# A decoder layer on one core: four low halves of the expert weights made by VectorE, and the last reads and stores issued from two queues

## What is computed

```python
x = x + attn(layernorm(x), Wq, Wk, Wv, Wo, betas)              # 16 heads of 128, segments of 64, delta memory
x = x + xattn(layernorm(x), ctx_512, Wq, Wkv_expand, Wout)     # 16 heads of 16, causal
x = x + ffn(layernorm(x), gate_kernel, w0, w1, wo)             # 8 experts of 512, the best 2 for each token

# ffn
top_k_weights, top_k_indices = top_k(x @ gate_kernel, 2);  weights = softmax(top_k_weights)
out = sum over the 2 experts of  weight * ((silu(x @ w0[e]) * (x @ w1[e])) @ wo[e])
```

## Time and profile before

| | us |
|---|---|
| median of 3 runs (lowest, highest) | 561.98 (561.61, 562.02) |
| the profiled execution | 559.13 |
| its span, first to last instruction | 557.4 |
| TensorE busy in the span | 498.6 (89%) |
| VectorE busy | 355.7 (64%) |
| ScalarE busy | 320.2 (57%) |
| GpSimd busy | 144.1 (26%) |
| mean granted TensorE clock | 0.954 of full |

### The profile page before, as it was taken

One profiled execution on the slowest core, in us unless ns is written; L12 is line 12 of the kernel. 1 busy time (PEld: TensorE's weight loads), 2 busy tenths in 40 slices (PEclk: granted clock), 3 DMA queues, 4 the chain that ended last, 5 costly groups with the idle time before them and its releaser, 6 DMA issues. The chain is left out here.

```text
span 557.4 us, 11832 instructions
## 1 busy us (share of the span) xinstructions
PE 498.6 (89%) x4164; PEld 417.9 (75%) x4165; DVE 355.7 (64%) x782; ACT 320.2 (57%) x762; POOL 144.1 (26%) x141
## 2 busy tenths in 40 slices
PE   8989999999999999999899799996737999999960
PEld 3768888887898888888689667774624888888850
DVE  5367777776654777776666377777372666666654
ACT  4377777778626777777672389996203444444430
POOL 5110000003100000000000439998011455555530
PEclk9989999999999999999999899999559999999995
DMA  9421111111010111120000024443213355454527
GB/s 266 160 57 44 55 55 55 56 58 58 19 39 20 56 47 53 55 56 20 0 2 1 1 82 148 145 135 101 68 41 113 119 169 168 144 157 152 169 76 226
DMA packets 24001, 48.05 MB, mean 86 GB/s; under 512 B 2960, under 2 KB 11168, under 8 KB 23968
## 3 DMA queue, kind: packets, MB, share of 16 engines
q1 hardware_dynamic: 21120, 41.17, 24.2%
q0 software_dynamic: 2240, 6.04, 3.1%
q10 hardware_dynamic: 608, 0.39, 0.3%
HBM read 42.48 MB, written 5.11 MB: 85 GB/s over the span
## 5 line engine op out<-in xcount | busy, mean ns | idle before, releaser
L666 PE MATMUL psum<-a_xt_hi,a_qk_hi 128*128 128x512 f32 x128 | 54.6, 426 | 0.0
L1409 POOL DMA_INDIRECT picks_dram<-x_wout,e_pick_row x23 | 38.8, 1685 | 51.8 <-DVE x_wout L1572 51.8
L666 PE MATMUL psum<-a_xt_hi,a_qk_lo 128*128 128x512 f32 x128 | 50.6, 395 | 0.0
L666 PE MATMUL psum<-a_xt_lo,a_qk_hi 128*128 128x512 f32 x128 | 50.5, 394 | 0.0
L987 ACT ACTIVATE x_probs<-psum,x_neg_max 128x128 f32<-128x128 f32 x128 | 45.9, 406 | 6.7 <-DVE x_neg_max L1044 6.7
L1450 ACT ACTIVATE e_inner_hi<-psum 128x512 fp32r<-128x512 f32 x23 | 13.8, 599 | 57.7 <-PE psum L1632 57.7
L578 DVE COPY a_weights_t<-psum 64x256 f32<-64x256 f32 x32 | 13.7, 428 | 49.4 <-PE psum L782 49.4
L916 POOL MEMSET x_mask<- 128x512 bf16 x1 | 0.5, 525 | 167.5 <-POOLq L250 167.5
L444 ACT ACTIVATE a_probs<-a_shifted 128x256 f32<-128x256 f32 x32 | 13.4, 419 | 50.1 <-DVE a_shifted L544 50.1
L796 PE MATMUL psum<-a_weights_t,a_v 64*128 64x64 f32 x256 | 34.9, 275 | 8.0 <-issue 4.1
L1623 PE MATMUL psum<-expert_w_hi,e_x_hi 128*128 x92 | 38.3, 416 | 2.2 <-DVE e_x_lo L1550 2.2
(11 more groups left out here) (238 smaller groups left out, 1513.5 us busy)
## 6 DMA issues: line engine op xcount, KB each, us to landing
x_k_t<-in_expert_wo SPq DMA_DIRECT2D x23, 512.0 KB, 3.5
a_qk_raw<-in_wqk SPq DMA_DIRECT2D x32, 256.0 KB, 2.6
x_xn_t<-in_expert_w SPq DMA_DIRECT2D x16, 512.0 KB, 3.8
a_wv_raw<-in_wv SPq DMA_DIRECT2D x17, 256.0 KB, 2.7
x_sb<-in_x SPq DMA_DIRECT2D x2, 512.0 KB, 5.0
x_k_t<-in_wo SPq DMA_DIRECT2D x1, 1024.0 KB, 10.4
x_v<-in_wo SPq DMA_DIRECT2D x1, 1024.0 KB, 12.9
xn_dram<-xn SPq DMA_DIRECT2D x1, 1024.0 KB, 4.4
```

The lines of the kernel that those rows point to most:

```text
L666: last = pe.matmul(out, pick_l(left[a], k), pick_r(right[b], k), start=start and n == 0, stop=n == 3 * KD - 1, skip_group_check=not start)
L1409: pool.indirect_dma_start(out=picks_dram, out_offset=bass.IndirectOffsetOnAxis(ap=pick_row[:, tile:tile + 1], axis=0), in_=y_rows[:, slot, ...
```

## The change

It does two things.

1. VectorE makes the low halves of pieces 3, 7, 11 and 14. The table `VECTOR_PIECES` says at the end of which batch's `step` it does so: 2, 3, 5 and 6. VectorE waits for the piece's high half first (`w_hi_ready`), and counts `w_split_v` up. GpSimd still casts all 16 pieces and skips the subtraction of these four. SP waits for `w_split_v` where the buffer was last used by one of them.
2. At the end SP issues the reads of the first picks and the stores of the even batches; ScalarE issues the reads of the second picks and the stores of the odd batches. Both wait for `y_stored` first.

```diff
--- before.py
+++ after.py
@@ -819,6 +819,7 @@
 NE_WIDTH = 2 * KD * M
 PIECE = NE_WIDTH // 2
 PIECES = 2 * NE
+VECTOR_PIECES = {3: 2, 7: 3, 11: 5, 14: 6}
 CROSS_SCALE = 1.0 / float(HD) ** 0.5
 CH = NX // 2
 ROWG = 32
@@ -875,7 +876,7 @@
     var3_ready, std3_ready, ln3_chain, xn3_ready = sem("e_var_ready"), sem("e_std_ready"), sem("e_ln_chain"), sem("e_xn_ready")
     xt3_done, xt3_ready, logits_done = sem("e_xt_done"), sem("e_xt_ready"), sem("e_logits_done")
     w_loaded = [sem(f"e_w_loaded{i}") for i in range(2)]
-    w_hi_ready, w_split = sem("e_w_hi_ready"), sem("e_w_split")
+    w_hi_ready, w_split, w_split_v = sem("e_w_hi_ready"), sem("e_w_split"), sem("e_w_split_v")
     inv_spread, t_first_ready = sem("x_inv_spread"), sem("x_t_first_ready")
     pv_done, inv_ready, heads_ready = sem("x_pv_done"), sem("x_inv_ready"), sem("x_heads_ready")
     it_done, it_ready, y_done, y_added = sem("x_it_done"), sem("x_it_ready"), sem("x_y_done"), sem("x_y_added")
@@ -894,6 +895,13 @@
         for b in range(B):
             step(b)
 
+    def vector_pieces(n):
+
+        return sum(1 for piece in VECTOR_PIECES if piece < n)
+
+    def piece_cols(n):
+        return slice(n * PIECE, (n + 1) * PIECE)
+
     def q_banks(pair):
 
         return [c.bank[4 + 2 * (pair % 2) + k][:, 0:2 * S] for k in range(KD)]
@@ -907,8 +915,10 @@
 
             sp.wait_ge(q_done, B // 2)
             for n in range(PIECES):
-                if n >= 2:
-                    sp.wait_ge(w_split, n - 1)
+                if n - 2 in VECTOR_PIECES:
+                    sp.wait_ge(w_split_v, vector_pieces(n - 1))
+                elif n >= 2:
+                    sp.wait_ge(w_split, n - 1 - vector_pieces(n - 1))
                 sp.dma_start(xn_t[:, n % 2, :], c.expert_w[n // 2][:, (n % 2) * PIECE:(n % 2 + 1) * PIECE]).then_inc(w_loaded[n % 2], 16)
 
         @block.gpsimd
@@ -949,11 +959,12 @@
             pad_values(0)
             pad_values(1)
             for n in range(PIECES):
-                cols = slice(n * PIECE, (n + 1) * PIECE)
+                cols = piece_cols(n)
                 pool.wait_ge(w_loaded[n % 2], 16 * (n // 2 + 1))
                 pool.tensor_copy(c.expert_w_hi[:, cols], xn_t[:, n % 2, :]).then_inc(w_hi_ready, 1)
-                pool.wait_ge(w_hi_ready, n + 1)
-                pool.tensor_tensor(c.expert_w_lo[:, cols], xn_t[:, n % 2, :], c.expert_w_hi[:, cols], ALU.subtract).then_inc(w_split, 1)
+                if n not in VECTOR_PIECES:
+                    pool.wait_ge(w_hi_ready, n + 1)
+                    pool.tensor_tensor(c.expert_w_lo[:, cols], xn_t[:, n % 2, :], c.expert_w_hi[:, cols], ALU.subtract).then_inc(w_split, 1)
                 if n >= 2 and n % 2 == 0 and n // 2 + 1 < B:
                     pad_values(n // 2 + 1)
 
@@ -1058,6 +1069,14 @@
                 if b >= 1:
                     normalise(b - 1)
                 copy_weights(2 * b, 0)
+                for n, at in VECTOR_PIECES.items():
+                    if at == b:
+                        split_piece(n)
+
+            def split_piece(n):
+                dve.wait_ge(w_hi_ready, n + 1)
+                dve.tensor_tensor(c.expert_w_lo[:, piece_cols(n)], xn_t[:, n % 2, :], c.expert_w_hi[:, piece_cols(n)],
+                                  ALU.subtract).then_inc(w_split_v, 1)
 
             def copy_weights(u, ch):
 
@@ -1352,6 +1371,8 @@
 
         return left is None or left >= n
 
+    picks = picks_dram[0:PICKS * P, :].rearrange("(k b p) d -> k p b d", k=TOPK, b=B)
+
     with nc.Block() as block:
         @block.sync
         def _(sp):
@@ -1372,12 +1393,10 @@
             tiles(sp, step)
             for slot in range(2):
                 sp.wait_ge(y_stored[slot], 16 * ((TILES + 1 - slot) // 2))
-            picks = picks_dram[0:PICKS * P, :].rearrange("(k b p) d -> p k b d", k=TOPK, b=B)
             for b in range(B):
-                for k in range(TOPK):
-                    sp.dma_start(picked[k][:, b, :], picks[:, k, b, :]).then_inc(gathered[b], 16)
-            for b in range(B):
-                sp.wait_ge(mixed, TOPK * (b - b % 2) + 3 + b % 2)
+                sp.dma_start(picked[0][:, b, :], picks[0, :, b, :]).then_inc(gathered[b], 16)
+            for b in range(0, B, 2):
+                sp.wait_ge(mixed, TOPK * b + 3)
                 sp.dma_start(out[b], c.x_sb[:, b, :]).then_inc(out_stored, 16)
             sp.wait_ge(out_stored, 16 * B)
 
@@ -1455,6 +1474,13 @@
                     split_wo(tile + 1, 1 - slot, pair + slot)
 
             tiles(act, step)
+            for slot in range(2):
+                act.wait_ge(y_stored[slot], 16 * ((TILES + 1 - slot) // 2))
+            for b in range(B):
+                act.dma_start(picked[1][:, b, :], picks[1, :, b, :]).then_inc(gathered[b], 16)
+            for b in range(1, B, 2):
+                act.wait_ge(mixed, TOPK * (b - 1) + 4)
+                act.dma_start(out[b], c.x_sb[:, b, :]).then_inc(out_stored, 16)
 
         @block.vector
         def _(dve):
```

## The result

The changed kernel takes 573.24 us (median of 6 runs, 565.58 to 574.57) against 562.0 (median of 6, 560.22 to 568.57). The ratio is 1.0167 with a 95% interval of 1.0116 to 1.0218: 9.4 us slower. The medians are of all executions, while a ratio leaves out those more than 1.5% above the fastest of their kernel, so it is not the quotient of the medians (1.0200). The profiled execution took 568.86 (span 567.1) against 559.13.

What follows compares the result with a forecast made beforehand. Each batch's pace was set by a ring of ScalarE's exponentials, TensorE's transposes and scores, and VectorE's maximum. Delay 10.8, normalisations -2.2, clock +3.0, reads and stores -1.4: +10.2 on 562.0 gives 572.2 us, range 566.6 to 577.

Steps and rivals of the forecast that it cites:

- The waits: Cross attention: VectorE waits for GpSimd's casts, 6.5 us at piece 7 and 2.6 at piece 14; +10.8 us in all.
- The clock behind the holes: TensorE, idle at batches 3 and 6, falls to half clock: +3.0 us (2.0 and 1.0), bounds 0 and 5.4.
- Piece 11: VectorE's subtraction at batch 5 meets no wait for its cast and adds 0.4 us.
- What comes back: End of cross attention: GpSimd stops before the normalisations, so the first is no longer slowed from 0.41 to 2.57 us; -2.2.
- a mere 1 us of the low end: Allowance for a routing stage with TensorE's clock up, lowering the range's bottom from 567.6 to 566.6 us.
- The reads and stores: Kernel's end: two issuing queues let transfers pack, 12.4 of the 13.9 us remain; -1.4 us, bounds 0 and -3.0.
- The sum: Whole kernel: +11.6 us for VectorE's pieces and -1.4 for the end give +10.2, on the median 562.0: 572.2.
- "faster": Rival: piece 7's cast is ready by batch 3 through hidden slack in the loads; 559.4 or 557.4 us, chance 0.05.
- "The clock holds": Rival: VectorE's waits in cross attention occur but TensorE keeps full clock; 569.2 us, chance 0.17.
- "The port": Rival: VectorE's and GpSimd's subtractions block each other, up to 2.4 us at two places; 577 us, chance 0.06.
- "The tail gives nothing": Rival: splitting the final reads and stores gains nothing; 573.6 us, inside the range, no chance of its own.

Runs made afterwards that it cites:

- the filled holes: Changed kernel plus 16 and 7 unused TensorE products where TensorE idles behind VectorE's two waits; ratio 1.0156 (1.0067 to 1.0245).
- last-piece: Kernel before, but VectorE makes the low half of piece 15 alone, behind its last normalisation; reads and stores as before; ratio 0.989 (0.9843 to 0.9937).
- filled runs: Kernel before plus unused TensorE products (3, 2, 2 and 4) in its idle times at the end of cross attention; ratio 0.9977 (0.9938 to 1.0015).

## Why the prediction was right

It said 572.2 within 566.6 to 577.0, and 573.24 was measured. Step by step, each time behind the block's start, before and after:

| step | before | after | delay | forecast |
|---|---|---|---|---|
| maximum, batch 4 | 40.48 | 47.80 | 7.3 | 7.4 |
| maximum, batch 5 | 48.16 | 56.70 | 8.5 | 9.4 with 2.0 of clock |
| maximum, batch 6 | 55.83 | 64.59 | 8.8 | 9.8 |
| maximum, batch 7 | 63.50 | 75.16 | 11.7 | 12.8 |
| first normalisation | 76.23 | 88.92 | 12.7 | 13.8 with 1.0 more |
| block's end | 90.00 | 98.44 | 8.4 | 11.6 |

- **The waits** (6.5 and 2.6 forecast, 6.73 and 2.61 measured) were right, and so was the reason: when the cast ends, and when VectorE arrives. For piece 7 both are rows of before. For piece 14 the 2.6 is in part luck: VectorE arrived 71.41 behind the block's start (forecast 70.44, without the prediction's own clock term), and the cast ended at 73.98 (forecast 73.04), since the late loop held GpSimd at `pad_values(5)` and `pad_values(6)` already, and not at `pad_values(7)` alone. Both ends were 1.0 too early, and the difference stood.
- **The clock behind the holes** was taken at 3.0 and is 2.3 (1.24 and 1.06, by the filled holes). Piece 11 cost 0.2 instead of 0.4.
- **What comes back** was taken at 2.2 and is 4.25: 12.69 of delay went in, 8.44 came out. The term that was mis-sized is the clock of the gate's products. I had it as a mere 1 us of the low end. Before, half clock lasted from 389.5 to the block's end, 10.9 us; in the changed kernel it lasted from 401 to 404.5 and again from 407.9 to 410.6, 6.2 us. So some 2 us of the 4.25 go with the clock, beside the 2.2 of the normalisations; the last-piece and filled runs show that 3.5 to 4.3 hang on it in all.
- **The reads and stores** were taken at 1.4 (the working shown, 13.9 - 12.4, gives 1.5) and gave 0.7. The transfers did pack closer, to 13.20 us, but VectorE's adds close the chain: it waits 0.24, 1.18 and 0.28 us between the first pairs and then runs without a gap to 564.94. The median from issue to landing rose from 2.7 and 3.1 to 4.2 and 5.3 us; the likely reason, not tested, is that the reads of the first batches now share the DMA engines with those of the last. Why the third batch comes as late as 559.73 was not settled.
- **The sum** was 3.2 too high in the block and 0.7 too low at the end. By the traces the change costs 8.4 - 0.7 = 7.7, beside 0.3 in the experts and 1.7 of clock ahead of it; by the ratio 9.4; the forecast was 10.2. That the median came within 1.0 us of 572.2 is partly luck: the executions' spread is as large as what separates these.

Of the rivals, "faster" failed at the point it named: `w_hi_ready` of piece 7 was 6.7 us late. "The clock holds" is false; it fell behind both holes, though its 569.2 lies inside the range too, and only the trace tells them apart. "The port" did not act here: the four subtractions took 1.21 to 1.23 us each, and one cast beside them 1.17 instead of 1.04. "The tail gives nothing" is 0.7 us off, which only the traces show.

## What to carry to other kernels

Before work is moved to another engine, write down when its input is ready and when that engine's list arrives at it; a wait in an in-order list costs the difference, for everyone behind it, while the engine that was relieved may only wait longer for its loads. Move the piece that stands in someone's way: here one subtraction of 16, made in an idle gap behind the critical work, gave a ratio of 0.989 where four in the middle gave 1.0167. And where single executions spread by 1%, read the length of a stage, with its clock beside it.

## What the runs showed that I had not expected

- Taking away a block of 2.2 us on VectorE shortened the stage by 5.7 us: before, TensorE idled 1.91 us behind it, was granted half meanwhile and kept half clock for the last 10.9 us (busy 9.5 of the last 10.0). In the changed kernel TensorE was granted half in the same stage without that block, got full clock back after 3.5 us of projection and transposes, and lost it once more during the last gate products. Which execution gets which is not explained here.
- The wait for loads had been covering a conflict: without it VectorE's subtractions of 1.22 us took 3.34, 2.02, 1.34 and 2.02.
- On two queues the core's DMAs moved 354 GB/s from 559 to 563 us, in the middle of the last stage; on one queue they moved 245 from 545 to 553 us, and 354 only in the two us after. Yet the end came only 0.7 us sooner.
